# Softmax sums and mean squares of the second layer moved to ScalarE with per-head exponentials, a buffer moved, and the order of all five queues written anew

## The chip, the cores and the metric

The kernel runs on one core of one Trainium2 chip. The metric is the device time of one execution in microseconds (us). PE is TensorE, DVE is VectorE, ACT is ScalarE, POOL is GpSimd, SP is SyncE, which here issues the DMAs.

## The reference

Two transformer layers follow one another on x of 4 x 1024 rows with D = 256. The first has a quantised self-attention, a quantised cross-attention over 77 context rows, and a GEGLU. The second has a cross-attention over the same 77 rows with rotary embedding, and a SwiGLU. Cut to what matters:

```python
# layer 0, H = 16 heads of 16; fq rounds to 8 bits
h1 = ln(x);  x = attn(h1, h1, dq1, dk1, dv1, dw1) + x        # 1024 keys per row and head
h2 = ln(x);  x = attn(h2, context, ...) + x                  # 77 keys: softmax over [., 77] per head
h3 = ln(x);  a, g = split(h3 @ ff_w1 + ff_b1);  x = a * gelu(g) @ ff_w2 + ff_b2 + x
# layer 1, 16 heads of 64, 4 key heads
h = x * rsqrt(mean(x**2) + 1e-6) * ln1_w
q, k = rope(h @ Wq), rope(kv @ Wk);  v = kv @ Wv
probs = softmax(q @ k.T / 8 + mask)                          # 77 keys per head
hidden = x + (probs @ v) @ Wo
x = hidden * rsqrt(mean(hidden**2) + 1e-6) * ln2_w
out = hidden + (silu(x @ Wgate) * (x @ Wup)) @ Wdown
```

## The kernel before, in words

The 4096 rows are 16 units of 256 rows. The program is a row of steps v = 0 to 17. In step v the large self-attention works on unit v, the chain "low" (rest of layer 0) on unit v-1, the chain "high" (layer 1) on unit v-2, and the chain "pre" (first norm and its three projections) on unit v+4. Steps 2 to 15 hold the attention and both chains, step 0 the attention and the setup of the context tables, step 1 the attention and low, step 16 low and high without attention rows, step 17 high alone. I call steps 2 to 15 the full steps.

The self-attention of a step is 32 row tiles of 128 x 1024 scores (`ROWT`), one for each head and half unit. Each goes around: PE fills `rowps` (L1419, two buffers), DVE reads it into a bias (`scaled_row`, L1038), ACT takes the exponential into `E` with its sum (L892), POOL makes the inverse (L733, L736), DVE rounds to `Pn` (L1056), a DMA transpose brings `PT`, and PE multiplies with the values (`outps`, L1446). A row's scores are filled two rows ahead; row n+2 needs the exponential of row n, since there are two `rowps`.

The two chains have short links. Their softmaxes over 77 keys come in four tiles of 128 rows x 8 heads x 77 = 616 numbers per unit and layer:

- low (`low_dve`): DVE finds the maxima (L1120) and subtracts them (L1126), ACT takes one exponential of 616 columns (L921), DVE sums it (L1103), inverts (L1104) and rounds (L1106), POOL widens (L777).
- high: DVE scales and masks (L1197), finds the maxima (L1202), POOL subtracts them (`less_max`, L791), ACT takes the exponential (L960), DVE sums (L1240, `high_sums`) and inverts (L1242), POOL multiplies (`probs`, L800).

The RMS norm of high runs as DVE batch statistics (L1061, L1065), four small POOL operations (L744, L746, L748, L753) and a DVE scaling (L1073). It occurs twice per unit: behind the residual `ffo` and behind the residual `pv1`. The norm of low is the same with mean and variance (scaling L1075, two POOL operations). SwiGLU writes half the gate to `hid1` (L972) and its tanh to `hid0` (L973), DVE multiplies with `up` (L1229), POOL multiplies the two (L823). Low's gate of GEGLU also goes to `hid0` (L938), and so waits until POOL is done with it.

All chains share three PSUM banks `work`. Nothing reorders at run time: each engine takes its turns in the order of a string in `TURNS` (e, i, r, b, n, t are the attention's turns; l, h, p, s the chains'), the same string in every step, and the banks follow PE's string.

## Time and profile before

| | |
|---|---|
| median of 3 runs | 2358.61 us (2352.96 to 2361.55) |
| the profiled execution | 2354.36 us, span 2352.6 us |
| busy: PE, DVE | 1904.7 us, 1828.8 us |
| busy: ACT, POOL | 1139.1 us, 946.6 us |
| mean granted TensorE clock | 0.889 |

The profile is of one execution. The span runs from its first to its last instruction, and the 1.8 us that are left lie around it. Busy time is what an engine spent executing, in all stages together.

### The profile page before, as it was taken

How to read it: one execution, taken by the hardware profiler on the slowest of the kernel's cores; microseconds unless marked ns; L12 is line 12 of the kernel's file. 1: busy time of each engine (PE TensorE's matmuls, PEld its weight loads, DVE VectorE, ACT ScalarE, POOL GpSimd, SP SyncE). 2: the span in 40 equal slices, each digit the busy share in tenths (PEclk: the TensorE clock that was granted, in tenths of full speed). 3: DMA queues.
4: the chain of work that ended last, by engine and by line, in shares of the span. 5: the costliest groups of instructions: out<-in, count | busy, mean ns of one | idle time of the engine just before them, and what ended most of it. 6: DMA issues, size and time to landing. Idle time of an engine off the chain costs nothing.

```text
span 2352.6 us, 35007 instructions
## 1 busy us (share of the span) xinstructions
PE 1904.7 (81%) x10552; PEld 1407.4 (60%) x10552; DVE 1828.8 (78%) x3327; ACT 1139.1 (48%) x1906; POOL 946.6 (40%) x1629
## 2 busy tenths in 40 slices
PE   4566577888889797989988897978797878878877
PEld 3223255666657575767766675756575655657665
DVE  1566769897988979798989889797979889795631
ACT  1244454656455554646564545555464645453221
POOL 1213335354543434453535435344444344352311
PEclk8667589999999898999999898989998988989998
DMA  7577444444535353434434453535444353433000
GB/s 232 122 137 139 87 85 98 74 91 82 101 76 101 77 122 67 87 78 88 99 69 104 77 117 72 98 68 102 69 85 82 70 109 68 89 63 63 1 11 5
DMA packets 658348, 203.77 MB, mean 87 GB/s; under 512 B 595388, under 2 KB 655536, under 8 KB 657904
## 3 DMA queue, kind: packets, MB, share of 16 engines
q1 hardware_dynamic: 654831, 201.52, 42.5%
q8 instruction: 86, 1.41, 0.3%
q14 instruction: 103, 0.84, 0.1%
q10 hardware_dynamic: 3328, 0.01, 0.1%
HBM read 43.76 MB, written 19.25 MB: 27 GB/s over the span
## 4 chain that ended last, share of the span: by engine, by line
DVE 41%; PE 35%; issue 11%; DMA 5%; SPq 3%; POOL 3%; ACT 2%; DVEq 0%; POOLq 0%; ACTq 0%
PE work L1364 15%; DVE scaled_row L1038 13%; PE work L1374 12%; DVE Pn L1056 7%; DMA PT<-Pn 4%; DVE scs L1197 2%; DVE scs L1126 2%; DVE nmx L1120 2%; PE outps L1446 2%; PE work L1357 2%; DVE st L1061 2%; DVE lsum L1240 1%; DVE hids L1150 1%; DVE hids L1183 1%; DVE lsum L1103 1%
## 5 line engine op out<-in xcount | busy, mean ns | idle before, releaser
L892 ACT ACTIVATE E<-rowps,ebias,der 128x1024 f32<-128x1024 f32 x512 | 616.6, 1205 | 692.4 <-DVE scaled_row L1038 595.5
L1038 DVE TENSOR_SCALAR_CACHE_REDUCE scaled_row<-rowps,der 128x1024 uint8<-128x1024 f32 x512 | 645.2, 1277 | 139.6 <-PE rowps L1419 136.8
L1056 DVE TENSOR_SCALAR Pn<-E,rowinv 128x1024 int16<-128x1024 f32 x512 | 418.9, 825 | 101.3 <-DMA PT<-Pn 81.6
L736 POOL TENSOR_TENSOR rowinv<-rowden,minus 128x1 f32<-128x1 f32 x512 | 336.0, 656 | 92.6 <-POOL rowden L733 90.1
L733 POOL TENSOR_TENSOR rowden<-rowsum,raw 128x1 f32<-128x1 f32 x512 | 136.5, 267 | 550.5 <-ACT E L892 547.7
L1419 PE MATMUL rowps<-KC,QP 16*128 16x512 bf16 x1024 | 178.8, 424 | 172.4 <-ACT E L892 159.9
L1364 PE MATMUL work<-hTs,ff_w_sb 128*128 128x256 f32 x1024 | 235.9, 387 | 1.2 <-ACT hTs L866 1.2
L1364 PEld LDWEIGHTS work<-hTs,ff_w_sb 128*128 128x128 f32 x1024 | 192.8, 192 | 36.6 <-issue 11.7
L1419 PEld LDWEIGHTS rowps<-KC,QP 16*128 16x128 bf16 x1024 | 39.0, 92 | 292.2 <-ACT E L892 194.6
L1374 PE MATMUL work<-VW,pTs 128*128 128x256 f32 x640 | 177.6, 437 | 3.4 <-ACT pTs L965 2.8
L1528 PE MATMUL work<-K,hids 128*128 128x154 f32 x1024 | 149.7, 300 | 17.6 <-DVE scs L1197 16.1
L1374 PEld LDWEIGHTS work<-VW,pTs 128*128 128x128 f32 x640 | 138.4, 223 | 32.9 <-ACT pTs L965 5.9
L1446 PE MATMUL outps<-PT,VB 128*16 128x256 f16 x2048 | 148.2, 292 | 10.9 <-DMA PT<-Pn 10.8
L1528 PEld LDWEIGHTS work<-K,hids 128*128 128x128 f32 x1024 | 136.4, 189 | 33.4 <-DVE scs L1197 25.3
L1364 PE MATMUL work<-hTs,Wgate_sb 128*128 128x256 f32 x512 | 148.8, 452 | 3.4 <-DVE scs L1126 2.2
L1364 PEld LDWEIGHTS work<-hTs,Wgate_sb 128*128 128x128 f32 x512 | 112.7, 229 | 33.9 <-DVE scs L1126 9.3
L1374 PE MATMUL work<-ff_w_sb,hids 128*128 128x256 f32 x512 | 118.1, 384 | 12.7 <-DVE hids L1150 12.7
L1446 PEld LDWEIGHTS outps<-PT,VB 128*16 128x16 f16 x2048 | 90.5, 94 | 62.6 <-issue 42.2
L1364 PE MATMUL work<-hTs,Wq_sb 128*128 128x256 f32 x512 | 119.8, 394 | 1.0 <-ACT hTs L864 1.0
L1364 PE MATMUL work<-hTs,Wup_sb 128*128 128x256 f32 x512 | 117.3, 382 | 2.0 <-ACT hids L973 1.2
L1374 PE MATMUL work<-Wdown_sb,hids 128*128 128x256 f32 x512 | 116.3, 386 | 2.4 <-POOL hids L823 2.4
L791 POOL TENSOR_TENSOR scs<-scs,nmx 128x616 f32<-128x616 f32 x64 | 80.5, 1258 | 91.6 <-ACT E L892 52.3
(143 smaller groups left out, 3126.1 us busy)
## 6 DMA issues: line engine op xcount, KB each, us to landing
PT<-Pn SPq DMA_TRANSPOSE x512, 3.1
VW<-vw_dram SPq DMA_DIRECT2D x8, 640.0 KB, 5.4
vw_dram<-scs SPq DMA_DIRECT2D x32, 154.0 KB
xa<-in_x SPq DMA_DIRECT2D x17, 256.0 KB, 3.1
QP<-q_dram SPq DMA_DIRECT2D x128, 32.0 KB, 2.1
oT<-OS SPq DMA_DIRECT2D x256, 16.0 KB, 1.8
xs<-in_x SPq DMA_DIRECT2D x16, 256.0 KB, 2.9
out<-xns SPq DMA_DIRECT2D x16, 256.0 KB, 2.5
```

Source lines behind the costliest of these rows:

```text
L733: nc.gpsimd.tensor_tensor(rowden[:, n:n + 1], rowsum[:, n:n + 1], raw[:, DW1:DW1 + 1], ALU.mult).then_inc(row_den.sem, 1)
L736: nc.gpsimd.tensor_tensor(rowinv[:, n:n + 1], rowden[:, n:n + 1], minus1[:], ALU.pow).then_inc(row_inv.sem, 1)
L791: nc.gpsimd.tensor_tensor(sc1[:, n], sc1[:, n], nmx[:, 1, n, :].unsqueeze(2).broadcast_to([P, 8, M]), ALU.add).then_inc(h_diff.sem, 1)
L892: nc.scalar.activation(E[:, slot, :], rowps[n % 2][:], ACT.Exp, bias=ebias[:, n:n + 1], scale=der[:, AL1:AL1 + 1], accum_out=rowsum[:, n:n ...
L1038: nc.vector.tensor_scalar(scaled_row[:, n % 2, :], rowps[n % 2][:], der[:, NAL1:NAL1 + 1], 3.0e38, ALU.mult, ALU.min, accum_out=ebias[:, n ...
L1056: nc.vector.tensor_scalar(Pn[:, place, :], E[:, ring(k)[0], :], rowinv[:, k:k + 1], 255.0, ALU.mult, ALU.min).then_inc(row_round.sem, 1)
L1061: ins = nc.vector.bn_stats(st[:, NT * layer + t, :], x[:, t, :])
L1364: ins = nc.tensor.matmul(ps[:, e * CH:(e + 1) * CH], w[:, c, (m0 + e) * P:(m0 + e + 1) * P], src[:, c, :], start=(c == 0), stop=(c == DC - 1))
L1374: ins = nc.tensor.matmul(ps[:, t * D:(t + 1) * D], src[:, c, t * P:(t + 1) * P], w[:, w0 + c, :], start=(c == 0), stop=(c == chunks - 1))
L1419: ins = nc.tensor.matmul(rowps[n % 2][:, e * (S // 2):(e + 1) * (S // 2)], QP[r:r + DH, p, t * P:(t + 1) * P], KC[r:r + DH, p, :], start=T ...
L1446: ins = nc.tensor.matmul(outps[quarter:quarter + DH, 0:CH], VB[:, kt, h * DH:(h + 1) * DH], PT[:, h % SLOTS, kt, :].bitcast(F16), start=(k ...
L1528: ins = nc.tensor.matmul(ps[:, e * 2 * M:(e + 1) * 2 * M], src[:, 4 * hf + mm, t * P:(t + 1) * P], K1[:, cs, g, :], start=(cs == 0), stop= ...
```

## The change

It has five parts.

1. The exponentials of the 77-key softmaxes are taken head by head: eight instructions of 77 columns in place of one of 616, each with an accumulated output that is the sum of the head. DVE's two sum reductions fall away. A turn of ACT holds four heads, so that a tile takes two turns.
2. In high the maxima are no longer subtracted by POOL. The exponential takes each head's negated maximum as its bias.
3. In high the mean of squares comes from ACT (`Square`, one instruction for each 128 rows, with accumulated output) in place of DVE's batch statistics. POOL has two small operations left in place of four.
4. The tanh of the gate goes into the place of high's scores (`hidg`) and no longer into `hid0`. Low's gate waits for PE's last reading of `hid0` as queries in place of POOL's SwiGLU product. High's first scores of the next unit now wait for that product.
5. The strings of all five engines are new, and SP's attention part is split into four kinds of turns (t, q, k, o).

```diff
     "step": {
         "DVE": (
-            "npbnpnbbhnnbbhnbnhnbhhhlnbhhhlnbhhbhnhhbssnbnshsnlbblnhhblnbnlbhnbhbblnnllnblllnnlbblnhbnlhbhlhn"
-            "bbnnnbblnhbnnbblll"),
-        "ACT": "eeepeeppeehpoeeeeohhelhhelehheehheeleoeeehllhhlehhlleleleelleolelleee",
+            "npnbbnpnbbhnbhnnbbhhhnhnlhhhbbhhnbblshhnnsbhnnbshnbsllbnnhhbbnllhbbhnllbnnblllnlbbnlnlhnblnlhhbb"
+            "hnnbnbbnlnhbbnlllb"),
+        "ACT": "eeeepeehpepohpeeheehheohhelehlhhhheeehhleelhlleoleheelllhhhhllleleeeloelellleee",
...
+        hidg = scs[:, 3:7].rearrange("p r h k -> p (r h k)")[:, 0:FC * CH].rearrange("p (m n) -> p m n", m=FC)
...
         def norm_scale(pool, u, layer, mv, va, rs, stats, rstd, n, rms):
-            if rms:
-                nc.gpsimd.tensor_tensor(va, mv[:, :, 0], mv[:, :, 0], ALU.mult).then_inc(rstd.sem, 1)
-                rstd.wait(pool, u, step + 1)
-                nc.gpsimd.tensor_tensor(va, va, mv[:, :, 1], ALU.add).then_inc(rstd.sem, 1)
...
+            nc.gpsimd.tensor_scalar(va, mv[:, :, 0 if rms else 1], RMS_EPS if rms else LN_EPS, 1.0, ALU.add, ALU.mult
+                                    ).then_inc(rstd.sem, 1)
+            rstd.wait(pool, u, 2 * n + 1)
             nc.gpsimd.tensor_tensor(rs, va, eps_half[:, 0:NT], ALU.pow).then_inc(rstd.sem, 1)
...
-            def less_max(n):
-                max_ready.wait(pool, u, n + 1)
-                nc.gpsimd.tensor_tensor(sc1[:, n], sc1[:, n],
-                                        nmx[:, 1, n, :].unsqueeze(2).broadcast_to([P, 8, M]),
-                                        ALU.add).then_inc(h_diff.sem, 1)
...
# low_act
-            for n in range(4):
-                yield
-                l_diff.wait(act, u, n + 1)
-                nc.scalar.activation(sc0[:, n % 3], sc0[:, n % 3], ACT.Exp, scale=der[:, AL2:AL2 + 1]).then_inc(l_exp.sem, 1)
+            for i in range(8):
+                yield
+                n, q = i // 2, i % 2
+                if q == 0:
+                    l_diff.wait(act, u, n + 1)
+                for h in range(4 * q, 4 * q + 4):
+                    ins = nc.scalar.activation(sc0[:, n % 3, h, :], sc0[:, n % 3, h, :], ACT.Exp,
+                                               scale=der[:, AL2:AL2 + 1], accum_out=lsum[:, 0, n % 3, h:h + 1])
+                if q == 1:
+                    ins.then_inc(l_exp.sem, 1)
...
                 if i == 0:
-                    silu_ready.wait(act, u - 1, 4)
+                    h_filled.wait(act, u - 1, item(HIGH_ITEMS, "sc1", 3) + 1)
...
# high_act
+            def mean_squares(n, x_ready):
+                yield
+                h_dve.wait(act, u, emptied("high", "D", x_ready))
+                y_out.wait(act, u, 0)
+                for t in range(NT):
+                    ins = nc.scalar.activation(xn1[:, t, :], x1[:, t, :], ACT.Square, scale=D ** -0.5,
+                                               accum_out=mv[:, NT + t, 0:1])
+                ins.then_inc(h_stats.sem, 1)
...
-            for n in range(4):
-                yield
-                h_diff.wait(act, u, n + 1)
-                nc.scalar.activation(sc1[:, n], sc1[:, n], ACT.Exp, scale=1.0).then_inc(h_exp.sem, 1)
+            for i in range(8):
+                yield
+                n, q = i // 2, i % 2
+                if q == 0:
+                    max_ready.wait(act, u, n + 1)
+                for h in range(4 * q, 4 * q + 4):
+                    ins = nc.scalar.activation(sc1[:, n, h, :], sc1[:, n, h, :], ACT.Exp, bias=nmx[:, 1, n, h:h + 1], scale=1.0,
+                                               accum_out=lsum[:, 1, n, h:h + 1])
+                if q == 1:
+                    ins.then_inc(h_exp.sem, 1)
...
# low_dve, high_sums
-                link(nc.vector.tensor_reduce(lsum[:, 0, n % 3, :], sc0[:, n % 3], AX.X, ALU.add))
                 link(nc.vector.reciprocal(rsum[:, 0, n % 3, :], lsum[:, 0, n % 3, :]))
...
-                nc.vector.tensor_reduce(lsum[:, 1, n, :], sc1[:, n], AX.X, ALU.add).then_inc(h_sums.sem, 1)
-                h_sums.wait(dve, u, n + 1)
                 nc.vector.reciprocal(rsum[:, 1, n, :], lsum[:, 1, n, :]).then_inc(recip_ready.sem, 1)
```

The strings move instructions at three places that the prediction speaks of. The first is ACT's queue in a full step, from high's first small exponential to its last; `scs` are the scores, `q` the quantised queries of low. Before:

```order
L960 ACTIVATE scs<-scs 128x616 x2
L892 ACTIVATE E,rowsum<-rowps,ebias,der 128x1024
L866 ACTIVATE hTs<-work,cols 128x256 x2
L960 ACTIVATE scs<-scs 128x616 x2
L892 ACTIVATE E,rowsum<-rowps,ebias,der 128x1024
L916 ACTIVATE q<-work,inv 128x512
L892 ACTIVATE E,rowsum<-rowps,ebias,der 128x1024
```

The same place in the changed kernel, where L885 is the row's exponential and L973 the small one of one head:

```order
L973 ACTIVATE scs,lsum<-scs,nmx 128x77 x4
L885 ACTIVATE E,rowsum<-rowps,ebias,der 128x1024 x2
L973 ACTIVATE scs,lsum<-scs,nmx 128x77 x8
L885 ACTIVATE E,rowsum<-rowps,ebias,der 128x1024
L895 ACTIVATE OS<-outps,der 128x256
L973 ACTIVATE scs,lsum<-scs,nmx 128x77 x8
L885 ACTIVATE E,rowsum<-rowps,ebias,der 128x1024
L859 ACTIVATE hTs<-work,cols 128x256 x2
L885 ACTIVATE E,rowsum<-rowps,ebias,der 128x1024
L973 ACTIVATE scs,lsum<-scs,nmx 128x77 x4
L909 ACTIVATE q<-work,inv 128x512
L973 ACTIVATE scs,lsum<-scs,nmx 128x77 x8
```

The four tiles, which stood in two places between rows, now lie in four places between rows, with four to twelve heads in each.

The second place is DVE's queue at low's last two softmax tiles. Before:

```order
L1120 TENSOR_REDUCE nmx<-work 128x4
L1126 TENSOR_TENSOR scs<-work,nmx 128x308 x2
L1103 TENSOR_REDUCE lsum<-scs 128x8
L1104 RECIPROCAL rsum<-lsum 128x8
L1106 SCALAR_TENSOR_TENSOR p<-scs,inv,rsum 128x616
L1103 TENSOR_REDUCE lsum<-scs 128x8
L1104 RECIPROCAL rsum<-lsum 128x8
L1106 SCALAR_TENSOR_TENSOR p<-scs,inv,rsum 128x616
```

In the changed kernel, where L1073 is the rounding of a row:

```order
L1132 TENSOR_REDUCE nmx<-work 128x4 x2
L1138 TENSOR_TENSOR scs<-work,nmx 128x308 x2
L1116 RECIPROCAL rsum<-lsum 128x8
L1118 SCALAR_TENSOR_TENSOR p<-scs,inv,rsum 128x616
L1116 RECIPROCAL rsum<-lsum 128x8
L1118 SCALAR_TENSOR_TENSOR p<-scs,inv,rsum 128x616
L1073 TENSOR_SCALAR Pn<-E,rowinv 128x1024
```

The reductions are gone and a row's rounding stands ahead of the last tile.

The third place is PE's queue at the gate projections of high, `Wgate_sb`. Before:

```order
L1419 MATMUL rowps<-KC,QP 128x512 x6
L1357 MATMUL work<-ident,xns 128x128 x4
L1474 MATMUL work<-K,q2T 128x308
L1419 MATMUL rowps<-KC,QP 128x512 x2
L1474 MATMUL work<-K,q2T 128x308
L1364 MATMUL work<-hTs,Wgate_sb 128x256 x12
L1446 MATMUL outps<-PT,VB 16x256 x16
L1364 MATMUL work<-hTs,Wgate_sb 128x256 x4
```

In the changed kernel:

```order
L1365 MATMUL work<-ident,xns 128x128 x4
L1427 MATMUL rowps<-KC,QP 128x512 x2
L1482 MATMUL work<-K,q2T 128x308
L1427 MATMUL rowps<-KC,QP 128x512 x2
L1482 MATMUL work<-K,q2T 128x308
L1372 MATMUL work<-hTs,Wgate_sb 128x256 x8
L1427 MATMUL rowps<-KC,QP 128x512 x4
L1372 MATMUL work<-hTs,Wgate_sb 128x256 x8
```

Half of the gate projections (8 of 16 matmuls) now stand ahead of two rows of scores that they stood behind.

## Rows read from the trace of the kernel before

**Rows 1.** The page's first part: span, busy time of each engine, share, instructions.
```profile
span 2352.6 us, 35007 instructions
...
PE 1904.7 (81%) x10552; PEld 1407.4 (60%) x10552; DVE 1828.8 (78%) x3327; ACT 1139.1 (48%) x1906; POOL 946.6 (40%) x1629
```

**Rows 2.** Windows by step: length, busy of PE, PEld, DVE, ACT, POOL, clock, DMA share, GB/s.
```profile
1097.40:1225.10 127.70, 113.01 (x648) 85.08 (x647) 112.10 (x204) 70.54 (x119) 59.80 (x101) 0.92 0.43 87
...
2135.10:2244.10 109.00, 90.20 (x466) 74.23 (x465) 56.85 (x112) 30.73 (x54) 29.46 (x39) 0.92 0.10 22
2244.10:2352.60 108.50, 79.93 (x352) 66.69 (x350) 29.75 (x59) 15.36 (x24) 17.25 (x20) 0.89 0.03 9
```

**Rows 3.** Line L943, the GELU table load, once in each unit: first and last start.
```profile
L943 ACT ACT_TABLE_LOAD  x16: 1283/1283/1283, 319.7 to 2244.1; - x16
```

**Rows 4.** Windows: two stretches of one full step, cut at starts of rows 8, 23, 8.
```profile
1136.00:1204.00 68.00, 55.88 (x332) 40.22 (x331) 65.18 (x118) 34.68 (x59) 32.20 (x51) 0.85 0.38 77
1204.00:1264.30 60.30, 57.73 (x319) 45.39 (x318) 47.43 (x88) 35.86 (x59) 26.66 (x50) 1.00 0.50 104
```

**Rows 5.** Chain of waits in the same two stretches, shares by line.
```profile
by line: DVE scaled_row L1038 23.4%; issue 13.4%; DVE Pn L1056 11.9%; DVE scs L1126 5.1%; DVE scs L1197 4.9%; DVE nmx L1120 4.8%; DVE lsum L1240 4.1%; DVE lsum L1103 3.4%; DVE p L1106 2.9%; PE work L1364 2.9%; PE work L1374 2.6%; DVE st L10
...
by line: PE work L1374 24.0%; PE work L1364 23.2%; DVE scaled_row L1038 12.7%; issue 10.6%; DVE Pn L1056 6.9%; DVE hids L1150 3.6%; PE outps L1446 3.2%; PE work L1357 2.8%; PE rowps L1419 2.4%; PE work L1489 2.1%; DVE hids L1183 1.3%; DVE s
```

**Rows 6.** Groups by line: DVE and POOL work that the change removes, wholly or in part.
```profile
L791 POOL TENSOR_TENSOR scs<-scs,nmx 128x616 f32<-128x616 f32 x64 | 80.5, 1258 | 91.6 <-ACT E L892 52.3 <-DVE nmx L1202 39.3
...
L1103 DVE TENSOR_REDUCE lsum<-scs 128x8 f32<-128x616 f32 x64 | 50.7, 792 | 5.8 <-DVE scs L1126 5.2 <-ACT scs L921 0.4
...
L1240 DVE TENSOR_REDUCE lsum<-scs 128x8 f32<-128x616 f32 x64 | 49.5, 773 | 0.0
...
L1061 DVE BATCH_NORM_STATS2 st<-xs 128x6 f32<-128x256 f32 x128 | 48.2, 418 | 2.2
```

**Rows 7.** Groups by line: ACT instructions of four widths, busy and mean ns.
```profile
L921 ACT ACTIVATE scs<-scs,der 128x616 f32<-128x616 f32 x64 | 49.7, 804 | 4.1 <-DVEq L1131 4.1
...
L960 ACT ACTIVATE scs<-scs 128x616 f32<-128x616 f32 x64 | 44.2, 713 | 47.5 <-POOL scs L791 47.5
...
L963 ACT COPY pTs<-work 128x512 f32<-128x512 f32 x32 | 18.6, 581 | 38.7 <-PE work L1537 38.7
...
L965 ACT COPY pTs<-work 128x256 f32<-128x256 f32 x32 | 12.0, 375 | 16.3 <-PE work L1537 16.1
```

**Rows 8.** Timeline of ACT around one row's exponential: start, length, instruction.
```profile
1024.04 1.19 ACT L892 ACTIVATE E<-rowps,ebias,der 128x1024 f32<-128x1024 f32 x1
1025.13 0.19 ACT L892 ACTIVATION_READ_ACCUMULATOR E<-rowps,ebias,der 128x1 f32 x1
1025.22 1.01 ACT L866 ACTIVATE hTs<-work,cols 128x256 f32<-128x256 f32 x2
```

**Rows 9.** Timeline at the mean squares behind `pv1`.
```profile
1179.01 0.75 DVE L1061 BATCH_NORM_STATS2 st<-xs 128x6 f32<-128x256 f32 x2
...
1179.91 0.25 DVE L1065 BATCH_NORM_AGGREGATE mv<-st 128x2 f32<-128x6 f32 x2
...
1181.79 0.70 POOL L753 TENSOR_TENSOR rs<-va,eps_half 128x2 f32<-128x2 f32 x1 [0.18 <-POOL va L748]
...
1182.52 0.62 DVE L1073 TENSOR_SCALAR xns<-xs,rs 128x256 f32<-128x256 f32 x2 [0.52 <-POOL rs L753]
```

**Rows 10.** Timeline: a POOL subtraction and the DVE scaling beside it.
```profile
1016.10 1.22 POOL L791 TENSOR_TENSOR scs<-scs,nmx 128x616 f32<-128x616 f32 x1 [1.18 <-DVE nmx L1202]
1016.22 1.57 DVE L1075 TENSOR_SCALAR xns<-xs,mv,rs 128x256 f32<-128x256 f32 x2
```

**Rows 11.** Line L1075: duration ns min/median/max, first and last start.
```profile
L1075 DVE TENSOR_SCALAR xns<-xs,mv,rs x64: 400/407/1348, 242.9 to 2232.7; 128x256 f32<-128x256 f32 x64
```

**Rows 12.** Who waited for whom: the longest entry, us, times, longest.
```profile
ACT E L892 <- DVE scaled_row L1038: 595.5, 274, 10.8
```

**Rows 13.** Timeline of the last step: POOL's first two probability tiles.
```profile
2293.89 2.39 POOL L800 TENSOR_TENSOR pps<-scs,rsum 128x616 f32<-128x616 f32 x2
```

More of the change, by code:

```diff
@@ L569, in attn_sync @@
-                quad = (n - LAG - 9) // 8
-                if (n - LAG - 9) % 8 == 0 and (parts["old"] if quad < 0 else parts["attn"]):
-                    output(quad)
+                for i in range(4):
+                    yield 2 * (21 + 2 * i) + 0.03
+                    if parts["more"]:
+                        if i == 0:
+                            qk_out.wait(sp, (v + 1) // PARTS * PARTS + PARTS - 1, qk_out.per)
+                            v_out.wait(sp, (v + 1) // PARTS * PARTS + PARTS - 1, v_out.per)
+                        keys(sp, v, 2, (i,))
```

125 lines of the change are left out of this document (56 added, 69 removed).

## The prediction

> **What bounds the kernel now.** I read the busy shares first. PE and DVE lead with 81% and 78% of the span, ACT has 48% and POOL 40% [rows 1]. Two engines near 80% can mean that both wait for each other or that they take turns, so the next view is the windows by step. A full step lasts 127.7 us, with PE busy for 113.0, DVE for 112.1 and ACT for 70.5 [rows 2]. The GELU table load comes once in each unit. From its first start at 319.7 [rows 3] to the border of the windows at 2135.1 [rows 2] lie 14 full steps, 129.7 us each.
>
> Cut at the right places, the step shows two regimes. From the start of row 8's exponential to that of row 23's it takes 68.0 us, and DVE is busy for 65.2 of them (96%), PE for 55.9 at a granted clock of 0.85, ACT for 34.7. From row 23 to row 8 of the next step it takes 60.3 us, with PE busy for 57.7 at the full clock and DVE for 47.4 [rows 4]. The chain of waits agrees. In the first stretch its eight largest DVE shares come to 60% and no PE group has over 3%; in the second the two projection lines of PE alone have 47% [rows 5]. So the first stretch is DVE's and the second PE's, and a DVE instruction is worth its time only in the first. Both sums are shares of this chain, and both reductions, L1240 and L1103, stand in it.
>
> **The change, part by part, for one full step.**
>
> *Sums off DVE.* Four reductions of 0.773 and four of 0.792 us [rows 6] come to 6.3 us. They all lie in DVE's stretch. **-6.3**
>
> *Mean squares.* Each of the two takes DVE 0.75 us of statistics and 0.25 of aggregation [rows 9]. The one behind `pv1` is in DVE's stretch and counts, the one behind `ffo` lies beside PE's work and I count it as nothing; if PE did not cover it, it would be 1.0 more, 14 us in all. **-1.0**
>
> *Waits of DVE.* Between statistics and aggregation 0.15 us pass, and the scaling waits 0.52 us for POOL [rows 9], whose four small operations become two. Before L1103 DVE stood for 5.2 us in 64 times, 0.3 in a step [rows 6]. **-1.0**
>
> *POOL's subtraction.* It takes 1.26 us four times in a step [rows 6]. It isn't in DVE's queue, but the pair of DVE scalings that began 0.1 us behind one of them took 1.57 us [rows 10]. The same operation has a median of 0.407 and a longest of 1.348 us [rows 11], so the pair would be 0.8. One such pair stands in every full step. **-0.7**
>
> *Gates moved on PE.* Eight of the 16 matmuls now stand two rows of scores earlier, in DVE's stretch, where PE has 12 us free [rows 4]. With the order's other moves this takes between 0 and 3.5 us out of PE's stretch. I take less than half, since it pays only where PE would not have waited there anyway. **-1.5**
>
> *Added on ACT.* No row shows an exponential of 77 columns. From 512 to 256 columns a copy falls from 581 to 375 ns, 0.80 ns a column. L921 has 804 ns at 616 columns [rows 7]; less 539 x 0.80 = 434 it is 0.37 us. For the accumulated output a second instruction follows. Behind the row's exponential it begins 0.10 us before the end, and the next instruction 0.09 after its start [rows 8]. So one head holds ACT for 0.37 - 0.10 + 0.09 = 0.36 us, if a short instruction overlaps as the long one does. From above it is bounded by the whole 256-column copy, 0.375, with 0.09 for the scale (L921 against L960, [rows 7]) and a reading of 0.19 with no overlap: 0.66. From below it is bounded by 0.27, if the reading hides altogether. I take 0.36, since it comes from the same kind of instruction in the same queue.
>
> All 64 heads of a step lie in DVE's stretch. There ACT has 34.7 us, loses 5.3 for the eight wide exponentials (3.2 and 2.8 by rows 7, less 0.1 of overlap each), and gains 64 x 0.36 = 23.0 and 0.75 for two squares. That is 53.2 us in a stretch that would now be about 59 long: ACT has room, but it is 90% busy and no longer 51%.
>
> The charge comes from the order. A row's exponential now queues behind blocks of four to twelve heads, and row n+2 of the scores waits for it, and DVE for the scores. Before, ACT stood for 595.5 us waiting for DVE [rows 12]; in this stretch it was free for (68.0 - 34.7)/15 = 2.2 us a row, and that is what a block can use up. A block of eight heads is 2.9 us long, and five places between rows hold eight or more. With the whole slack at each of them 0.7 us are left over, 3.5 in a step; with half of it 1.8 us, 9 in a step; with two rows' slack nothing. DVE has roundings in pairs at these places, which it can do meanwhile. So between 0 and 9 I take **+2.5**, near the first of these values.
>
> The Trainium skill speaks of this price on its page "ScalarE: Activation LUTs", section "What ACT_TABLE_LOAD costs": an ACTIVATE with immediates has 186 ns of fixed cost, a pointer operand adds 93, and neighbours overlap by 93. It gives no price for reading the accumulator. An estimate by that page alone is 0.25 us a head, and ACT would have 46 us in the stretch; a block of eight would fit in the slack, the charge of 2.5 would be 1 at most, and the time 20 us less. Rows 8 show the reading as an instruction of its own, so I don't follow it.
>
> The sum is -6.3 - 1.0 - 1.0 - 0.7 - 1.5 + 2.5 = **-8.0 us** for a full step, 121.7 in place of 129.7, and 14 x 8.0 = 112 us.
>
> *Elsewhere.* Step 1 has low's sums only, -3. In the last two steps PE is busy for 90.2 and 79.9 us of 109 and DVE for 56.9 and 29.8 [rows 2]: each link of the chain counts, and no DVE time as such. A mean square saves about 1 us there (POOL's last operation begins 1.6 us after the aggregation [rows 9]; two operations and their hops go). POOL's first two probability tiles begin at 2293.9 [rows 13] behind four subtractions of which they need two, 1.3 each, while the exponentials they wait for grow. I take -4 for both steps. The setup holds none of this.
>
> Together 112 + 3 + 4 = 119 us. The profiled execution took 2354.4 us and the median of the runs is 2358.6, 4 us above. The sum gives 2354 - 119 = 2235 for the profiled execution and **2240 us** for the median, 5% below before. A measurement of this kernel can tell about 0.5%, 12 us, from no change.
>
> A second rule of the skill bears on PE's stretch. The page "Perfetto Trace Analysis", section "Identifying the Most-Contended Engine", says that matmul busy time overstates TensorE and that the weight loads show its headroom. By it PE has room in its own stretch (weight loads busy for 45.4 of 60.3 us, [rows 4]), which then also is a chain of waits, and the mean square behind `ffo` would count too. The chain in rows 5 has PE's matmuls on it, so the sum leaves this out. I give it 0.15 of the chances, inside the forecast's own, since 2226 lies in its range.
>
> **The rivals.**
>
> *The row loop takes DVE's place.* ACT does not bind by its sum but by its order: a row's exponential that stands behind eight to twelve heads holds back two rows of scores. For it speaks that the slack of 2.2 us a row is a mean, and need not lie where the blocks do. Against it speaks that DVE has much work of its own between rows, 65.2 us over 15 rows, 4.3 each [rows 4]. With the charge at its upper bound a step gains 10.5 - 9 = 1.5 us, so 21 + 7 = 28 us in all: about 2330, still below before.
>
> *ACT becomes the bound, and it is slower.* If short accumulating exponentials don't overlap, 0.66 a head, ACT has 34.7 - 5.3 + 42.2 + 1.3 = 72.9 us of work in a stretch that took 68.0. With the share that DVE left idle (3 us) the stretch is 76, less 1.5 from PE's: +6.5 a step, 91 in all, less 7: about 2440. It decides from the head at which ACT alone fills 68.0: 0.36 + (68.0 - 53.2)/64 = 0.59 us. Against it speaks the overlap in rows 8.
>
> *ACT ties with DVE, and nothing changes.* The same mechanism with a head of 0.56 us gives ACT 66.5 us of work and a stretch of 69.5, +1.5 for the stretch and -1.5 for PE's: about 2352. This is also where it would come out if the change didn't do what it says, that is if the reductions were only traded for waits on the same exponentials.
>
> **How the numbers follow.** The forecast has 0.68, the row loop 0.18, no change 0.06, ACT as the bound 0.08. Its own range goes from 2190 (a charge of 0 and 2.5 from the gates: 11.5 a step, 168 in all) to 2290 (a charge of 6: 4.5 a step, 70 in all). The range of 8 in 10 is **2190 to 2335**: it takes in the row loop and leaves out the other two cases and a little below. Faster by over 0.5%: the forecast and the row loop, 0.86. Within 0.5%: 0.06. Slower: 0.08.
>
> **What would show it.** Right: full steps of 121 to 122 us; DVE busy for about 104 in each (112.1 - 6.3 - 2.0) and ACT for 89 to 90; the small exponentials one by one at about 0.36 us from start to start; DVE still over 90% busy from row 8 to row 23, now about 60 us; PE's stretch 59; the granted clock of the first stretch above 0.85. Wrong: heads at over 0.5 us from start to start, ACT over 95% busy in the first stretch, or DVE's scaled rows waiting there for PE and PE for ACT's exponential by more than 3 us a step. The forecast would be too high if PE's stretch fell well under 58 us.

## The result, and the profile after

The changed kernel takes **2302.39 us** (median; 2297.88 to 2304.84) against 2359.28 for the kernel before on the same chip: a ratio of 0.976, 95% interval 0.9745 to 0.9776. It is 57 us faster. The forecast had 2240, 119 us faster, with a range of 2190 to 2335: the direction and the range held, and the gain came to less than half of the size that was forecast (57 of 119 us).

The profiled execution took 2297.88 us, with a span of 2296.1. Its busy shares and its chain, to be read beside [rows 1]:

```profile
PE 1856.2 (81%) x10552; PEld 1387.1 (60%) x10552; DVE 1716.8 (75%) x3071; ACT 1414.1 (62%) x3954; POOL 820.0 (36%) x1501
...
PE 53%; ACT 14%; DVE 14%; issue 8%; DMA 4%; SPq 4%; POOL 2%; DVEq 0%; POOLq 0%; ACTq 0%
```

The work went where the forecast said: DVE has 112 us less, ACT 275 more, POOL 127 less. In the chain of the kernel before DVE had 41% and PE 35%; now PE has 53%.

The small exponentials in ACT's queue (start, duration), as the first tile of high begins:

```profile
1117.43 0.36 ACT L973 ACTIVATE scs<-scs,nmx 128x77 f32<-128x77 f32 x1 [10.10 <-DVE nmx L1214]
1117.70 0.19 ACT L973 ACTIVATION_READ_ACCUMULATOR scs<-scs,nmx 128x1 f32 x1
1117.79 0.34 ACT L973 ACTIVATE scs<-scs,nmx 128x77 f32<-128x77 f32 x1
1118.04 0.19 ACT L973 ACTIVATION_READ_ACCUMULATOR scs<-scs,nmx 128x1 f32 x1
1118.13 0.34 ACT L973 ACTIVATE scs<-scs,nmx 128x77 f32<-128x77 f32 x1
```

One head follows the other after 0.36 and 0.34 us. ACT had stood for 10 us ahead of this tile. The two stretches of the same step as in [rows 4], again cut at row 8's and row 23's exponential:

```profile
1106.00:1173.80 67.80, 54.06 (x332) 40.40 (x331) 61.04 (x113) 51.80 (x187) 25.80 (x48) 0.90 0.44 82
1173.80:1231.30 57.50, 54.59 (x318) 42.62 (x317) 44.31 (x76) 35.84 (x64) 25.24 (x45) 1.00 0.56 103
```

The columns are those of [rows 4]. DVE has 4.1 us less work in the first stretch (61.0 against 65.2), and the stretch is as long as before: 67.8 against 68.0. The second one went from 60.3 to 57.5. Over all full steps, cut at the starts of the rows' exponentials, the first stretch has a mean of 68.4 (before 68.6) and the second 57.9 (61.0). A step, taken from row 0 to row 0 of the next, has 126.4 (129.8, mean of 13). The 14 full steps together gave 48 us. I had expected 112.

### The profile page after: what moved, and what is told of

It reads as the page before. It is cut to its first block, busy times and chain, and to the rows that moved or that the text cites. A ratio compares the mean times of both kernels' runs of the same rounds, so it can differ in the third digit from the quotient of the medians.

```text
span 2296.1 us, 36528 instructions
## 1 busy us (share of the span) xinstructions
PE 1856.2 (81%) x10552; PEld 1387.1 (60%) x10552; DVE 1716.8 (75%) x3071; ACT 1414.1 (62%) x3954; POOL 820.0 (36%) x1501
## 4 chain that ended last, share of the span: by engine, by line
PE 53%; ACT 14%; DVE 14%; issue 8%; DMA 4%; SPq 4%; POOL 2%; DVEq 0%; POOLq 0%; ACTq 0%
PE work L1372 23%; PE work L1382 19%; DVE scaled_row L1055 5%; ACT scs L973 5%; PE work L1536 3%; DMA PT<-Pn 3%; ACT E L885 3%; PE rowps L1427 2%; DVE Pn L1073 2%; ACT scs L918 2%; PE outps L1454 1%; PE work L1365 1%; ACT hTs L859 1%; SPq L542 1%; PE work L1497 1%
## 5 line engine op out<-in xcount | busy, mean ns | idle before, releaser
L885 ACT ACTIVATE E<-rowps,ebias,der 128x1024 f32<-128x1024 f32 x512 | 615.0, 1202 | 377.3 <-DVE scaled_row L1055 312.6
L1073 DVE TENSOR_SCALAR Pn<-E,rowinv 128x1024 int16<-128x1024 f32 x512 | 417.4, 826 | 108.1 <-DMA PT<-Pn 66.1
L748 POOL TENSOR_TENSOR rowden<-rowsum,raw 128x1 f32<-128x1 f32 x512 | 122.8, 240 | 889.1 <-ACT E L885 886.0
L751 POOL TENSOR_TENSOR rowinv<-rowden,minus 128x1 f32<-128x1 f32 x512 | 309.0, 603 | 92.0 <-POOL rowden L748 88.4
L973 ACT ACTIVATE scs<-scs,nmx 128x77 f32<-128x77 f32 x512 | 176.1, 351 | 176.3 <-DVE nmx L1214 176.3
L918 ACT ACTIVATE scs<-scs,der 128x77 f32<-128x77 f32 x512 | 175.9, 347 | 5.3 <-DVEq L1143 5.3
L1382 PE MATMUL work<-VW,pTs 128*128 128x256 f32 x640 | 162.2, 401 | 7.3 <-DVE pTs L1219 4.6
L1372 PE MATMUL work<-hTs,a_wq_sb 128*128 128x256 f32 x256 | 97.0, 546 | 63.2 <-ACT hTs L859 63.2
L1382 PEld LDWEIGHTS work<-VW,pTs 128*128 128x128 f32 x640 | 123.0, 201 | 38.8 <-ACT pTs L981 14.3
L1536 PE MATMUL work<-K,hids 128*128 128x154 f32 x1024 | 141.3, 296 | 1.4 <-DVE hids L1194 1.4
L1372 PE MATMUL work<-hTs,Wq_sb 128*128 128x256 f32 x512 | 128.8, 409 | 10.9 <-ACT hTs L857 10.9
L1372 PEld LDWEIGHTS work<-hTs,Wq_sb 128*128 128x128 f32 x512 | 102.6, 205 | 34.1 <-issue 19.4
```

What stands on the lines that cost most here:

```text
L748: nc.gpsimd.tensor_tensor(rowden[:, n:n + 1], rowsum[:, n:n + 1], raw[:, DW1:DW1 + 1], ALU.mult).then_inc(row_den.sem, 1)
L751: nc.gpsimd.tensor_tensor(rowinv[:, n:n + 1], rowden[:, n:n + 1], minus1[:], ALU.pow).then_inc(row_inv.sem, 1)
L885: nc.scalar.activation(E[:, slot, :], rowps[n % 2][:], ACT.Exp, bias=ebias[:, n:n + 1], scale=der[:, AL1:AL1 + 1], accum_out=rowsum[:, n:n ...
L918: ins = nc.scalar.activation(sc0[:, n % 3, h, :], sc0[:, n % 3, h, :], ACT.Exp, scale=der[:, AL2:AL2 + 1], accum_out=lsum[:, 0, n % 3, h:h ...
L973: ins = nc.scalar.activation(sc1[:, n, h, :], sc1[:, n, h, :], ACT.Exp, bias=nmx[:, 1, n, h:h + 1], scale=1.0, accum_out=lsum[:, 1, n, h:h ...
L1073: nc.vector.tensor_scalar(Pn[:, place, :], E[:, ring(k)[0], :], rowinv[:, k:k + 1], 255.0, ALU.mult, ALU.min).then_inc(row_round.sem, 1)
```

## The experiments

Each kernel was run beside the kernel before on the same chip, and each ratio is to that. "8 to 23" and "23 to 8" are the mean lengths of the two stretches over the full steps of the profiled execution. The kernel before had medians from 2354.7 to 2360.0 us beside the different kernels, so a difference between two kernels below, taken of their medians, can be off by 3 us or so. The ratios are free of this.

| kernel | median, us | ratio (95%) | 8 to 23 | 23 to 8 |
|---|---|---|---|---|
| before | 2359.28 | | 68.6 | 61.0 |
| after | 2302.39 | 0.976 (0.9745 to 0.9776) | 68.4 | 57.9 |
| e1_wide | 2278.98 | 0.9655 (0.9639 to 0.9671) | 67.1 | 58.6 |
| e2_between | 2302.01 | 0.9758 (0.9742 to 0.9774) | 68.2 | 58.1 |
| e3_old_order | 2455.2 | 1.0406 (1.0387 to 1.0424) | 74.9 | 61.8 |
| e4_gate_hid0 | 2326.74 | 0.9862 (0.9848 to 0.9877) | 68.6 | 59.5 |
| e5_before_no_sums | 2317.72 | 0.9828 (0.9807 to 0.9848) | 65.9 | 61.2 |
| e6_old_order_wide | 2293.31 | 0.9731 (0.9713 to 0.9749) | 65.3 | 60.9 |
| e7_pe_less | 2278.49 | 0.9659 (0.9634 to 0.9684) | 68.9 | 56.4 |
| e8_sums_dve | 2358.46 | 1.0003 (0.9988 to 1.0017) | 71.9 | 58.6 |
| e9_gates_early | 2346.66 | 0.9964 (0.9952 to 0.9977) | 70.9 | 58.7 |
| e10_before_no_sub | 2302.21 | 0.9774 (0.9761 to 0.9788) | 64.9 | 61.3 |
| e11_squares_dve | 2342.02 | 0.9943 (0.9929 to 0.9957) | 69.1 | 59.3 |
| e12_tr0_early | 2302.35 | 0.9776 (0.9757 to 0.9794) | 68.2 | 58.0 |
| e13_last_tile_wide | 2304.2 | 0.9783 (0.9765 to 0.98) | 68.2 | 58.1 |
| e14_before_sums_twice | 2459.93 | 1.0442 (1.0425 to 1.0459) | 74.3 | 61.8 |
| e15_before_no_high_sums | 2338.1 | 0.9923 (0.9907 to 0.9939) | 67.2 | 61.2 |
| e16_two_orders | 2301.24 | 0.9765 (0.9751 to 0.9778) | 68.3 | 58.2 |

### What the heads cost, and what the order is worth

**e1_wide**: one exponential for each tile, no sums anywhere.

```diff
-                for h in range(4 * q, 4 * q + 4):
-                    ins = nc.scalar.activation(sc0[:, n % 3, h, :], ..., accum_out=lsum[:, 0, n % 3, h:h + 1])
+                if q == 1:
+                    nc.scalar.activation(sc0[:, n % 3], sc0[:, n % 3], ACT.Exp, scale=der[:, AL2:AL2 + 1]
+                                         ).then_inc(l_exp.sem, 1)
```

> The changed kernel with one exponential of 616 columns for each small softmax tile in place of eight of 77, and with no sums at all (the reciprocals read a constant; the maxima are not subtracted in layer 1, whose scores are scaled down): the softmax sums are left out. ACT loses 64 x 0.35 - 6 = 16 us in a full step. Theory A, the blocks of small exponentials hold up the row loop in the first stretch: that stretch shrinks from 68 to about 61 and the kernel comes to 2302 - 14 x 6.5 = about 2210. Rival B, PE's unbroken run of projections and scores between rows 8 and 10 sets the stretch: 2302 - 14 x 1.5 = about 2280.

Measured: 2278.98. The heads cost 23 us in all, where I had 35 (2.5 in each of 14 steps). The first stretch is 1.3 us shorter and the second 0.8 longer; theory A had 7 off the first.

**e2_between**: rows 9 and 10 of the attention ahead of high's scores on PE and DVE, and ahead of the first heads on ACT. High's chain comes later by that much.

```diff
-  DVE  8:"bhhhnhnlhhh" 9:"b"    10:"bhhn"      ACT  8:"eh" 9:"e" 10:"ehh"
+  DVE  8:"bhhhn"       9:"bhnl" 10:"bhhhhhn"   ACT  8:"e"  9:"e" 10:"ehhh"
-  PE   9:"rhhllhhhhh" 10:"rvv"
+  PE   9:"rhhll"      10:"rhhhhhvv"
```

> The changed kernel with rows 9 and 10 of the attention moved ahead of layer 1's scores on PE and DVE, and ahead of the first small exponential on ACT; nothing else differs. Theory A2: ACT stands 10 us in each step before the first small exponential and then has 18 us of work with PE waiting; two row exponentials and their biases moved into the hole take 2.5 us from each full step: 2302 - 35 = about 2267. Rival: the rows only move, what follows is set by the small exponentials' own chain, 2300 +- 8.

Measured: 2302.01, nothing. The waits (in us in total, times, longest) show why. In the change, and below it in this kernel:

```profile
ACT E L885 <- DVE scaled_row L1055: 312.6, 161, 10.8
ACT scs L973 <- DVE nmx L1214: 176.3, 16, 14.9
```

```profile
ACT E L881 <- DVE scaled_row L1051: 445.9, 170, 10.8
...
ACT scs L969 <- DVE nmx L1210: 35.0, 16, 15.6
```

Most of the 10 us of each step in which ACT stood before the first head are gone (141 us in all), and ACT stands for 133 us more before the rows' exponentials. ACT waited for DVE in either place.

**e3_old_order**: the code of the change with the strings of the kernel before, adapted to the new number of turns.

> The changed code in the order of before (same turns of PE and DVE, each small exponential's turn doubled on ACT, the POOL subtractions left out, SP's turns at the rows where they were). If the new strings carry the gain, this is slower than the changed kernel: ACT then has 16 small exponentials, 5.6 us, in a row in front of row 11 and 16 more ahead of row 12, and it comes to 2330 to 2350. If the instructions moved off DVE carry it, this is 2302 +- 8.

Measured: 2455.2, slower than before by 4%, and 105 us above the end of the 2330 to 2350 that I had expected.

**e6_old_order_wide**: the same, with the wide exponentials of e1 and no sums.

> The changed code in the order of before, with wide exponentials and no sums: the one difference to the run with the old order (2455) is the 64 small exponentials of a step. If these cost what they do only where the order leaves ACT no hole, this is 150 to 190 us faster than that run, 2265 to 2305, although the same edit was worth 23 us in the new order. If the old order is slow for another reason (the mean squares on ACT, the new waits), it stays above 2400.

Measured: 2293.31. So in the old order the heads cost 162 us, and in the new one 23. The new order in turn is worth 153 us with the heads and 14 without. The first stretch in the old order with the heads (e3), columns as above:

```profile
1176.40:1251.50 75.10, 55.29 (x326) 39.41 (x325) 57.16 (x106) 51.34 (x183) 26.04 (x45) 0.82 0.37 68
```

No engine is busy for more than 57.2 of the 75.1 us there. ACT has the same work as in the change, and the stretch is 7 us longer. In e3 sixteen heads stand in a row behind the exponentials of rows 10 and 11. From row 10 to 11 and from row 11 to 12 it takes 4.3 us more each than in e6 (means over the full steps), about what sixteen heads (5.5 us) have above two wide exponentials (1.4), and behind row 21, where low has such a block, 2.8 more. It is the mechanism of my first rival, a row's exponential behind a block of heads, and the new strings take it away.

### What the sums were worth

**e5_before_no_sums**: the kernel before, without DVE's eight sums.

```diff
-                link(nc.vector.tensor_reduce(lsum[:, 0, n % 3, :], sc0[:, n % 3], AX.X, ALU.add))
...
-                nc.vector.tensor_reduce(lsum[:, 1, n, :], sc1[:, n], AX.X, ALU.add).then_inc(h_sums.sem, 1)
-                h_sums.wait(dve, u, n + 1)
```

> The kernel before, in its own order, without DVE's eight sums of a step (L1103, L1240; the reciprocals read a constant, so the softmax sums are left out). If a microsecond of DVE in the first stretch is a microsecond of the kernel, as the prediction had it, 6.3 us go from each full step and 3 from step 1: 2359 - 91 = about 2268. If the order fixed on PE takes it back, less than half of that: 2320 or above.

Measured: 2317.72, so 39 us, where the forecast had counted 6.3 x 14 and step 1's, 91. This is the largest miss. The piece from row 20's exponential to row 22's shows how, in one step. Before, with the columns as above:

```profile
1186.70:1198.00 11.30, 9.87 (x36) 6.72 (x38) 10.65 (x20) 7.49 (x14) 2.54 (x4) 0.69 0.40 78
```

and without the sums:

```profile
1169.60:1180.90 11.30, 9.94 (x36) 7.04 (x38) 9.10 (x17) 7.45 (x13) 3.65 (x7) 0.65 0.39 77
```

DVE has three instructions and 1.55 us less, and the time is the same to the digit; over the full steps the mean is 11.5 before and 10.9 without the sums, so 0.6 us came off. In the chain of before, from 1186 to 1198, nearly all of it was DVE's, L1103 with a fifth (a piece that reaches over an end of the window counts whole, so the shares come to over 100%):

```profile
by line: DVE Pn L1056 19.6%; DVE lsum L1103 19.4%; DVE p L1106 16.6%; DVE scs L1126 14.6%; DVE nmx L1120 10.6%; DVE scaled_row L1038 10.0%; issue 8.3%; DVE rsum L1104 5.3%; DVEq L1131 0.3%; DVEq L154 0.2%
```

and without the sums it is PE's, 24 matmuls of the gates in 7.16 us:

```profile
by line: PE work L1361 63.4%; PE rowps L1416 10.1%; PE work L1354 9.3%; ACT E L891 7.2%; PE work L1471 5.5%; issue 5.2%
```

PE had been there all the time, busy for 9.87 of 11.30 us at a granted clock of 0.69. In the whole stretch DVE is now idle for 6.2 us. The two longest waits are half of it (us in total, times, longest; the stretch 1119.6 to 1186.0 of this kernel):

```profile
DVE rsum L1102 <- ACT scs L920: 1.6, 1, 1.6
DVE pTs L1205 <- PE work L1534: 1.5, 1, 1.5
```

**e14_before_sums_twice**: the same eight sums, each done twice.

> The kernel before with each of DVE's eight sums done twice, so 6.3 us of DVE's time more in a full step and the same output. Taking the sums away gave 39 us of 91. Theory (the order of before is fitted to its work: DVE holds as far as it is now, and with less work other waits take over at once, with more work it holds in full): about +90 us, 2440 to 2460. Rival (a part of the sums always lies beside something else, in both directions): about +40 us, 2395 to 2405.

Measured: 2459.93, 104 us more. One full length more of the sums (91 us) costs all of it and a little over; one length less gives 0.43 of it. DVE was the bound, but the sums' removal could get only 39 us from it.

**e15_before_no_high_sums**: the kernel before without the sums of the second layer alone.

> The kernel before without the sums of the second layer (DVE L1240) and with those of the first (the sums are left out, so the output is another). Forecast's terms: 3.2 us a step, 46 us, 2313. Both sorts together gave 39 us. If the two sorts lie at separate places and give the same share each: 2338 to 2340. If only low's counted: 2355. If high's alone reached the next limit: 2320 to 2325.

Measured: 2338.1. High's sums give 18 us, and so low's the other 21. They stand in different rows, and of each sort a little over 0.4 of its length counts.

**e8_sums_dve**: e1_wide with the sums back on DVE, that is the sums in the new order.

> The changed kernel in its new order, with wide exponentials on ACT and the eight sums of a step back on DVE (the maxima are not subtracted in layer 1, whose scores are scaled down, which leaves POOL's part out). Against the run with wide exponentials and no sums (2279) it has only the 6.3 us of DVE more. If DVE still binds somewhere in the first stretch: 2279 + 14 x 3 to 6 = 2320 to 2360. If PE's order holds the time, 2279 to 2295, and the sums on ACT would have bought nothing in this order.

Measured: 2358.46, 80 us above e1_wide. The new order is written for a DVE without sums. With them it is as slow as the kernel before, though it has neither POOL's subtraction nor high's mean squares on DVE.

### The other parts

**e10_before_no_sub**: e5 with POOL's subtraction (L791) taken away too.

> The kernel before without DVE's sums and also without POOL's subtraction of the maxima (both sorts of work are left out, so the output is another). With the sums alone taken away it took 2317.7 us, and its chain between rows 11 and 13 ran through POOL's subtractions and products. Theory (POOL's queue at rows 11 to 13 is what holds in the stretch once DVE's sums are gone): four subtractions of 1.26 us go, and DVE's scalings no longer share with them, 1.0 to 1.5 us a step: about 2300. Rival (the order of the strings holds, not POOL): under 0.4 us a step, 2312 to 2318.

Measured: 2302.21, 16 us less than e5 by the medians and 13 by the ratios, as the theory had it. The forecast's term was 10 (0.7 x 14). From here to e6_old_order_wide, the mean squares and the gate's place in the old order, only 9 us are left (10 by the ratios).

**e4_gate_hid0**: the change with the gate's tanh in `hid0` again.

```diff
-                nc.scalar.activation(hidg[:, 2 * i:2 * i + 2, :]..., ps[:], ACT.Tanh, scale=0.5
+                nc.scalar.activation(hid0[:, 2 * i:2 * i + 2, :]..., ps[:], ACT.Tanh, scale=0.5
...
-                    h_filled.wait(act, u - 1, item(HIGH_ITEMS, "sc1", 3) + 1)
+                    silu_ready.wait(act, u - 1, 4)
```

> The changed kernel with the gate's tanh back in hid0 and low's gate waiting for POOL's product again. Theory: the wait ends before ACT comes to it (the product's turn on POOL is one row earlier), 2302 +- 8. Rival: the place was what let PE's stretch shrink from 60.5 to 57.7 us: up to 2302 + 14 x 2.8 = 2341.

Measured: 2326.74, so 24 us, most of it (1.7 a step) in the second stretch. The wait is there, 4.4 us in a step, and in the change no wait of low's gate for POOL is left:

```profile
ACT hids L938 <- POOL hids L816: 66.7, 15, 4.7
```

So my theory was wrong and the rival right in kind. The forecast had no term for the place of the gate.

**e11_squares_dve**: the change with the mean squares back on DVE, and four small operations on POOL.

```diff
+                for t in range(NT):
+                    ins = nc.vector.bn_stats(st[:, NT + t, :], x1[:, t, :])
...
+                for t in range(NT):
+                    ins = nc.vector.bn_aggr(mv[:, NT + t, :], st[:, NT + t, :])
```

> The change with the mean squares of the second layer taken by DVE's statistics again, with the four small operations of POOL behind them, and nothing else undone. The forecast put 1.0 us of DVE's time and 1.0 of its waits in a step on this, with 1 us twice at the end: 2302 + 28 + 2 = 2332. If the norm behind the residual of the feed-forward, in PE's stretch, counts too: 2345. Rival (both norms stand where DVE has something else to do or PE covers them): 2302 to 2310.

Measured: 2342.02, 40 us, near the case in which both norms count. The second stretch has 1.4 us a step of it, the first 0.7, and what follows on the last row's exponential 9 in all (213.9 against 204.9 us). PE's wait for the normed rows, in the change and here:

```profile
PE work L1365 <- DVE xns L1184: 55.2, 22, 3.9
```

```profile
PE work L1379 <- DVE xns L1198: 84.3, 32, 5.8
```

PE waits 29 us more. The two norms were not put back one by one, but the second stretch holds only the norm behind the feed-forward's residual, and 0.8 of its 1.4 us stand between rows 5 and 6, next to it. So this norm, which I had counted as nothing, is on the path in the stretch that I gave to PE.

**e7_pe_less**: the change with half of the matmuls of GEGLU's first projection left out, by leaving one of two contraction chunks away. The expectation counts 16 matmuls in a unit, 3.6 us, for them. It is 32 of 64, as the two profiles show, the change above and e7 below (count, then busy us and mean ns of one, then PE's idle time before them and who ended it):

```profile
L1372 PE MATMUL work<-hTs,ff_w_sb 128*128 128x256 f32 x1024 | 234.2, 388 | 9.8 <-ACT hTs L859 9.8
```

```profile
L1372 PE MATMUL work<-hTs,ff_w_sb 128*128 128x256 f32 x512 | 135.6, 418 | 28.7 <-ACT hids L938 18.9
```

That is 98.6 us of this group in all, 6.2 in a step.

> The changed kernel with one of two contraction chunks of the GEGLU projections left out (half of that product, 16 of 32 matmuls of 0.23 us in a unit, 3.6 us of PE in the second stretch). Theory: PE runs there without a gap and sets the step, so all of it comes off: 16 x 3.6 = 58 us, 2302 - 55 = about 2247. Rival: the step is set by the softmax chains and rows, and it moves by under 20 us.

Measured: 2278.49, 24 us, a quarter of the group's time. Over the full steps the second stretch, where these matmuls stand, is 1.4 us shorter, and the first 0.5 longer. In the second stretch PE is busy for 48.7 us in place of 53.5, and idle for 7.7 in place of 4.4. All of PE's busy time fell by 67.3 us (1856.2 to 1788.9) and not by 98.6: the other matmuls, unchanged in number, took 1653.3 us in place of 1622.0, 1.9% more, and the mean granted clock fell from 0.900 to 0.883, by 1.9%. Even in its own stretch PE's work counts by less than half.

### Places in the new order

**e9_gates_early**: behind row 22 two gate tiles ahead of low's last tile.

```diff
-  ACT 22:"elllhhhhlll"
+  ACT 22:"elhhllhhlll"
```

> The change with one edit: on ACT behind row 22's exponential two of high's gate tiles are evacuated ahead of the eight heads of low's last tile, not behind them. In the profile of the change PE stands for about 0.4 and 0.7 us in a full step at the banks that these gates hold. Theory (the order of ACT's queue around the heads sets when banks come free, and each such wait of PE counts): about 1 us less a step, 2288 us. Rival (PE only meets the next wait, and low's last tile is late by two gates, 2.3 us): no change or up to 1 us a step more, 2302 to 2316.

Measured: 2346.66, 44 us slower, where the rival had 14 at most: DVE's reciprocal of the tile begins 7.9 us behind the start of row 22's exponential in place of 5.4, and this delay of 2.5 us costs 3.5 in each step. In the waits of the change and of this kernel:

```profile
DVE rsum L1116 <- ACT scs L918: 5.2, 16, 0.7
```

```profile
DVE rsum L1112 <- ACT scs L914: 45.8, 16, 6.0
...
PE work L1485 <- POOL pps L780: 36.5, 16, 5.8
```

DVE waits 2.9 us in a step for the heads, then PE 2.3 for the tile; the gap behind row 22 grows by 2.4 us and the one behind row 23 by 1.2. PE's waits of 0.4 and 0.7 us at the gates, which I wanted to save, were the cheaper choice.

**e12_tr0_early**: low's evacuation `tr0` in the middle of the eight heads behind row 11. (They are the second half of high's second tile and the first half of its third, and not its first tile, as the expectation says.)

```diff
-  ACT 11:"eohh"  12:"el"
+  ACT 11:"eohlh" 12:"e"
```

> The change with one edit: on ACT the evacuation of low's transposed rows (tr0) stands between the two halves of high's first tile of heads behind row 11, not behind all eight and row 12's exponential. In the profile of the change PE stands 3.8 us there in a full step, and low's next projection on PE then runs at the lower clock (3.75 us). Theory (a head block in front of an evacuation costs PE its length, 1.4 us for half a tile and 1.3 for the row's exponential, and the clock besides): 2 to 3 us less a step, about 2265 us. Rival (row 12's exponential and the second half come later by the evacuation and DVE waits for them in turn): within 5 us of 2302.

Measured: 2302.35, nothing, though the wait that I saw fell to its half. In the change and here:

```profile
PE work L1372 <- ACT hTs L859: 72.9, 36, 3.8
```

```profile
PE work L1368 <- ACT hTs L855: 35.1, 36, 1.5
```

PE's eight matmuls behind this evacuation (`a_wq_sb`) also take 78.5 us in all in place of 97.0; in the change's step they run from 1131.1 to 1134.9, mostly in the window with a granted clock of 0.51 that stands under e16. So PE is relieved of 38 us of waiting and 18 of work in this stretch, and nothing comes of it. The gaps behind rows 12 and 13 are 2.3 us shorter together (means over the full steps), those behind rows 11, 14 and 15 are 2.1 longer, and from row 16 on all is as in the change.

**e16_two_orders**: both edits, e2's and e12's. (In e2's it is the rows that come earlier, and high's turns that come later; the expectation has it the other way round.)

> The change with the edits of e2 and e12 together: high's projections one row earlier on PE and DVE, and low's evacuation between the two halves of high's first tile on ACT. Each alone gave nothing, though each took a wait of 2 to 10 us away where it stood. Theory (the two places cover each other, and either alone only moves the wait to the other): together 2 us less a step, about 2275 us. Rival (both only bring forward work whose result is not late, and DVE and ACT, each over 90% busy from row 9 to row 13, hold there): within 5 us of 2302.

Measured: 2301.24, nothing. The two waits don't cover each other. The windows of the change in these rows show what is busy there:

```profile
1118.00:1122.00 4.00, 3.02 (x45) 1.97 (x43) 3.73 (x7) 3.66 (x12) 0.74 (x2) 1.00 0.00 0
1122.00:1126.00 4.00, 3.62 (x26) 3.18 (x24) 4.00 (x10) 4.00 (x19) 1.93 (x5) 1.00 0.51 72
1126.00:1130.00 4.00, 0.98 (x6) 0.51 (x6) 3.96 (x7) 4.00 (x20) 2.32 (x4) 1.00 0.03 6
1130.00:1134.00 4.00, 2.90 (x7) 2.39 (x8) 3.58 (x6) 3.51 (x13) 2.69 (x4) 0.51 0.67 126
```

For 16 us DVE is busy for 15.3 and ACT for 15.2, and PE for 10.5. That moving a turn there only changes who goes first is my reading of these windows.

**e13_last_tile_wide**: low's last tile alone wide on ACT and summed on DVE.

> The change with low's last tile alone back to one wide exponential on ACT and a sum on DVE, in the same order. In the profile of the change ACT works without a gap for 10 us in front of row 23's exponential, and these eight heads are 2.8 us of it; delaying the same tile by 2.3 us cost 3.5 us a step. Theory (there ACT's queue sets the time, not DVE's): ACT 2.1 us shorter, DVE 0.8 longer where it has just waited 0.3 for the heads; 1 to 2 us less a step, 2275 to 2290 us. Rival (DVE's 0.8 us counts and ACT's 2.1 doesn't): 2302 to 2313 us.

Measured: 2304.2, nothing. ACT is done with the tile 3.4 us behind the start of row 22's exponential in place of 5.4, and row 23 is no earlier (11.4 us behind row 22 in place of 11.3). But the tile itself isn't earlier either: with the sum in front of it, DVE's reciprocal begins at 5.9 us in place of 5.4. So ACT's queue alone does not set row 23, and what an earlier tile would give is not tested. The rival, DVE's 0.8 us counting, had 2302 to 2313, and 2 us can't be told from nothing.

No version of these that computes the whole reference beats the change by more than can be told.

## Why the prediction was wrong in its size

**The bound (DVE in the first stretch, PE in the second).** The busy shares and the chain were read rightly, and e14 confirms that DVE held the first stretch. What I drew from it, "a DVE instruction is worth its time only in the first", passed silently over to "in the first it is worth all of its time". That is the step that failed. PE's 55.9 us at a clock of 0.85 stood in the same stretch, unevenly spread. DVE's idle time in this stretch of this one step shows the limit behind: 2.8 us before, then 6.2 in e5 and e10 and e6 alike. With the sums gone DVE waits for PE, ACT and POOL within the same rows, and of the 6.3 us that were to come off each step 2.7 came off the first stretch (68.6 to 65.9).

**Sums off DVE, -6.3 a step.** 39 us against 91 in the order of before (e5). On the way from before to after by single parts, below, this term carries 50 of the 62 us by which the forecast was off.

**Mean squares and their waits, -2.0 a step.** In the new order 40 us, against 30 in the forecast (28, and 2 at the end): under-counted, since the norm in PE's stretch counts too (e11). In the old order it came to 9 or 10 together with the gate (e10 to e6). In the forecast this stood as a bound that I did not take, and as what would follow from the page "Perfetto Trace Analysis" of the Trainium skill, section "Identifying the Most-Contended Engine". The page says that matmul busy time is no good measure of how close TensorE is to its limit, and has its headroom judged by the weight loads; that busy time overstates it is my wording, not the page's. By this rule PE has headroom in its stretch (weight loads for 45.4 of 60.3 us). By e7 (24 us off for 99 us of matmuls) and e11 the runs agree with it, and 0.15 was too little for it.

**POOL's subtraction, -0.7 a step.** 13 to 16 us in place of 10 (e10).

**Gates moved on PE, -1.5 a step.** The new order without the heads gives 14 us (e6 to e1; 18 by their ratios), and 21 were forecast. By the stretches it takes 2.3 from the second and adds 1.8 to the first: so what left PE's stretch was not free in DVE's, as I read it.

**Heads on ACT, 0.36 us each.** Right: 0.34 to 0.36. Bounded by 0.27 and 0.66 from the trace of before, the middle value came out, because the accumulator's reading there overlapped the same way. The page "ScalarE: Activation LUTs" of the Trainium skill, section "What ACT_TABLE_LOAD costs", would have given 0.25, and the measurement decides against it for this form.

**The charge of +2.5.** 23 us against 35 (e1). Right in kind and too high, and as far as the profiles show it isn't where I put it. Of the 13 us between the two profiled executions, the time after the last row's exponential has 11 (204.9 against 193.8), and a full step differs by 0.4 us. But the profiled execution of the change was the fastest of its four and that of e1 the slowest, so where the other 10 us between the medians lie is not shown.

**What was left out.** The gate's new place, 24 us (e4). I described the wait that it takes away and gave it no term. The expectation of e4 had even set down that the wait ends before ACT comes to it, and it does not.

**Steps 0, 1 and the end.** Step 1 gave 4.5 us (3 forecast), the time after the last row 2.2 (4 forecast): the mean squares gain 9 there and the heads cost 11, beside smaller parts.

One way from before to after by single parts, with each ratio laid on 2359:

| step | runs | measured | forecast |
|---|---|---|---|
| sums off DVE | before to e5 | -41 | -91 |
| POOL's subtraction | e5 to e10 | -13 | -10 |
| mean squares, and the gate's place | e10 to e6 | -10 | -30 |
| the new order | e6 to e1 | -18 | -21 |
| the heads | e1 to after | +25 | +35 |
| the rest of the end | | 0 | -2 |
| sum | | -57 | -119 |

Each of these steps depends on the order in which it is made. In the new order the sums are worth 80 (e8), the mean squares 40 (e11) and the gate's place 24 (e4). The old order was fitted to the old work and the new one to the new, and a term measured in one isn't worth the same in the other.

**The rivals.** The row loop at 2330 had the nearest time, with the first stretch unchanged as it foretold. Its mechanism is real, 162 us in the old order (e3 against e6), but in the change it is not the cause: without the heads altogether the stretch is only 1.3 us shorter. That its time came nearest is luck. ACT as the bound, and the tie, fell with the price of a head: ACT is busy for 51.8 of 67.8 us.

**What the profile should have shown.** ACT at 87.6 us in a step (89 to 90 foretold) and DVE at 105.4 (104) came close, and the heads and the clock in the first stretch (0.90) were as foretold. The first stretch at 60 us was not; it is 68. I had named DVE over 90% busy there as a sign, and 61.0 of 67.8 is just 90%, but that sign could not tell 60 us from 68.

**What stays open.** What holds the first stretch in the change. Four edits of the order and of one tile (e2, e12, e13, e16) gave nothing. The windows under e16 speak for DVE and ACT together. The chain of waits in this stretch speaks more for PE, which had no group above 3% there before:

```profile
by line: PE work L1372 17.8%; PE work L1382 16.1%; ACT scs L973 11.4%; PE work L1536 7.8%; DVE scaled_row L1055 7.8%; ACT E L885 6.5%; ACT scs L918 6.1%; issue 5.3%; DVE Pn L1073 2.9%; PE work L1545 1.8%; PE rowps L1427 1.8%; ACT hids L989
```

Over all 14 first stretches PE has 46% of the chain, ACT 25% and DVE 18%; before, DVE had 70% and PE 9%. Against PE as the one limit speaks e12, which relieves it there for nothing; against ACT speaks e1, which takes 16 us of work from it in this stretch and makes it 1.3 us shorter. No run takes work from both DVE and ACT, or matmuls from PE in this stretch.

## What to carry to other kernels

An engine that is 96% busy bounds a stretch, but the gain from relieving it ends at the next engine. Before counting an instruction at its length, look in its own rows at who is second, and how near: here 1.55 us less of DVE's work took 0.6 us off, in one step nothing, where PE was busy for 87% of the same time. Doubling a suspected cost tells whether it binds, and only removing it tells what it is worth; here the two gave 104 and 39 us. Where the order is written by hand, a part of a change has no price of its own: judge code and order together, and expect the new code in the old order to be slower (here 4%) even if both together are faster.

## What the runs showed that I had not expected

- Work taken from PE came back in part as a lower granted clock: without matmuls that had taken 99 us the mean clock is 0.883 in place of 0.900, the other matmuls take 31 us more, and 24 us are gained (e7).
- The granted clock in the second stretch varies between steps with the same instructions, and the stretch with it. Two successive steps of e8, columns as above:

```profile
1202.20:1263.90 61.70, 58.79 (x318) 45.16 (x318) 44.32 (x76) 35.81 (x64) 25.29 (x45) 0.93 0.50 96
1335.10:1393.60 58.50, 55.59 (x319) 43.34 (x318) 44.33 (x76) 35.82 (x64) 25.30 (x45) 0.99 0.45 91
```

At 0.93 the stretch takes 3.2 us more, all of it in PE's busy time, while DVE, ACT and POOL have the same to do.
- More can be lost than a delay is long: the last low tile 2.5 us later costs 3.5 us a step (e9). Taking 2 us of work on it from ACT gave nothing, where DVE got 0.8 more and the tile was 0.4 us later (e13).
